# A context attention that takes its value products on four column tiles and its row sums on GpSimd

## The chip, the cores and the metric

The kernel runs on one core of one Trainium2 chip. The metric is the device time of one execution in microseconds, the median of several runs; lower is better. Each kernel is also executed once under the hardware profiler.

## What is computed

A decoder of four layers on x (4 x 256 x 128) with a context of 4 x 1601 x 96. Each layer has a self attention, a context attention and a feed-forward part, all in float32. The change touches only layer 0's context attention. Its eight heads of width 128 attend over all 4 x 1601 = 6404 context places for all 1024 queries, since the split into heads joins the batches:

```python
def _split_heads(t):
    b, n, _ = t.shape
    t = t.reshape(b, n, HEADS, DIM_HEAD)
    return t.transpose(2, 0, 1, 3).reshape(HEADS, b * n, DIM_HEAD)
...
sim = jnp.einsum('hid,hjd->hij', qh, kh) * SCALE
mean = jnp.mean(sim, axis=-1, keepdims=True)
sim = (sim - mean) * ATTN_MATRIX_SCALE + mean
attn = jax.nn.softmax(sim, axis=-1)
out = jnp.einsum('hij,hjd->hid', attn, vh)
...
return jnp.einsum('bni,iq->bnq', out, Wout) + bout
```

The mean shift drops out of the softmax; what is left is a softmax of 1.5 times the scaled scores, times the values, times Wout, added to x.

## The kernel before

The program is one list of stages. A stage (`Core.stage`) is a block in which every engine has its own hand-written instruction list; stages are separated by a barrier of all engines. Inside a stage the engines are held together by semaphores alone, and each engine takes its list in order.

`fold_weights` (L1112) multiplies, for each head, Wq with Wk and Wv with Wout, so that the big stage works on the 96 raw context features: `fold_q` turns a normalised x into a query over the context features, `fold_v` turns a mixture of context rows into the output. `ContextAhead` (L1145) holds the context in SBUF twice: as columns in thirds of 32 features, four tiles of places stacked on the 128 partitions (`c1`), and as rows, 128 places by 96 features and a 97th column of ones (`rows1`), which a memset (L1159) prepares.

`attend_all_places` (L829) is one stage. Its units of work:

- A **block** is one head and one half of the queries (512): 16 blocks. A **unit** is a block and one part of the context tiles (tiles 0 to 23 or 24 to 50): 32 units. A **group** or **slot** is four tiles of 128 places of one unit: 6 slots in the first unit of a block, 7 in the second, 208 in all. The last slot of a block has only two full tiles and one of 4 places.
- In slot s TensorE makes the **scores** of group s (L871): 12 products, four row tiles of the array side by side (32 features each) times three thirds, into banks 0 to 3. Every float32 product is two passes. ACT copies them to the **ring** of 11 slots in SBUF (L977). DVE keeps a running **maximum** over the tiles of the unit (L1039) and at its end folds it (L1045, L1047).
- The maxima are turned by TensorE (L882), reduced by DVE (L1051), spread again over all partitions by TensorE (L888) and placed by ACT (L946). Nine slots behind the scores (LAG) DVE adds them to the ring, the **shift** (L1020, L1024); ACT takes the **exponential** in place (L963).
- One slot later TensorE makes the **values** (L901): for each tile four products with 128 exponentials-by-queries as weights (loaded into the array) and the 97 columns of the rows streaming, summed over the unit in bank 4 or 5. The 97th column gives the row sums. A product of zeros (L898) opens each bank.
- At the end of a block DVE brings the two units to a common maximum, adds them and divides by the sums (L1069 to L1081), TensorE turns the result (L909), ACT copies it (L987), TensorE multiplies it by `fold_v` (L915, **mix**), DVE adds it to x (L1088).
- The three thirds of the next block's query are made (L854, L859) and copied (L953, L957) in slots 5 and 6 of a block, in banks 6 and 7.

GpSimd has no work in this stage. The order on TensorE within a slot is: scores, spread, queries, mix, values, turn of the maxima, turn of the result:

```python
for s in range(len(GROUP) + LAG + 3):
    if s < len(GROUP):
        score(s)
    ...
    if 0 <= s - LAG - 1 < len(GROUP):
        values(s - LAG - 1)
```

Two other places of the kernel matter for the prediction. In layer 0's self attention, `rotate` (from L602) multiplies query and key pieces of 128x256 by tables, eight on GpSimd (L612) and eight on DVE (L618) in the same stage, both from SBUF and with no wait between the two streams; then DVE adds them (L622). The value products of the self attention (L394) have 32 output rows each, at partitions 0, 32, 64 and 96 of one bank, and the exponentials of four heads streaming; ACT writes those exponentials at L419. In layer 2's context attention GpSimd adds 128x1601 tiles (L2780, L2785) and copies them (L2787) while DVE takes the eight largest of a row (L2810).

Of the kernel before, what the change touches and what calls it, by code (L numbers as in the profile page):

```python
# [806 lines left out]
CW = CD + 1  # L807
QUERY_AFTER = [sum(LAST[u] + 3 < FIRST[2 * n - 2] + 5 for u in range(UNITS)) for n in range(BLOCKS)]
TURN_AFTER = [1 + sum(FIRST[2 * n] + 5 <= LAST[u] + 1 for n in range(BLOCKS - 1)) for u in range(UNITS)]
# [19 lines left out]
def attend_all_places(k, c1, rows1, fold_q, fold_v, bufs):  # L829
# [4 lines left out]
    ring, top, folded_top, neg, low, spread_top, q1, first_sums, part, y, yT, gap, recip, zeros = bufs  # L834
    with k.stage() as (block, signal):
# [3 lines left out]
        evacuated, own, combined, y_turned, y_placed, mixed, added = (signal() for _ in range(7))  # L839

        @block.tensor
        def _(pe):
            def thrice(n, part):
                return fold_q[:, n // 2, part, :]

            def query(n):
                if n >= 3:
                    pe.wait_ge(added, n - 2)
                if n:
                    pe.wait_ge(query_placed, 3 * n)  # L850
                if n > 1:
                    pe.wait_ge(placed, QUERY_AFTER[n])
                for part, bank in enumerate((7, 6)):
                    pe.matmul(k.ps[:, bank, :], thrice(n, part), k.zT[:, (n % 2) * 512:(n % 2 + 1) * 512],  # L854
                              start=True, stop=True).then_inc(queried, 1)

            def query_rest(n):
                pe.wait_ge(query_placed, 3 * n + 1)
                pe.matmul(k.ps[:, 7, :], thrice(n, 2), k.zT[:, (n % 2) * 512:(n % 2 + 1) * 512],  # L859
                          start=True, stop=True).then_inc(queried, 1)  # L860
# [15 lines left out]
            def turn(u):  # L876
                pe.wait_ge(folded, u + 1)
                if u:
                    pe.wait_ge(placed, u)
                pe.wait_ge(query_placed, 3 * TURN_AFTER[u])  # L880
                for a in range(4):
                    mm = pe.transpose(k.ps[:, 6, a * P:(a + 1) * P], folded_top[:, a * P:(a + 1) * P], k.ident[:])  # L882
                mm.then_inc(turned, 1)

            def spread_out(u):
                pe.wait_ge(negated, u + 1)
                for a in range(4):
                    mm = pe.transpose(k.ps[:, 6, a * P:(a + 1) * P], neg[:, u % 4, a:a + 1].broadcast_to([P, P]), k.ident[:])  # L888
# [16 lines left out]
            def turn_rows(n):  # L905
                pe.wait_ge(combined, n + 1)
                pe.wait_ge(query_placed, 3 * min(n + 3, BLOCKS))
# [12 lines left out]
            for s in range(len(GROUP) + LAG + 3):  # L920
# [13 lines left out]
                for u in range(UNITS):  # L934
                    if s == LAST[u] + 1:
                        turn(u)
# [2594 lines left out]
```

## Time and profile before

| | |
|---|---|
| median of 3 runs | 6041.28 us (6040.34 to 6050.42) |
| the profiled execution | 6040.86 us, span 6039.1 us |
| TensorE, matmul / weight loads | 4169.8 us (69%) / 2653.2 us (44%) |
| DVE, ACT, GpSimd | 3423.9 (57%), 1894.8 (31%), 255.7 (4%) us |
| mean granted clock of TensorE | 0.82 |

The span is the time between the first and the last record of the profiled execution. Busy time counts an engine's instructions, overlapping ones once; the mean of an instruction is its own length, so that products that run side by side have means that add up to more than the busy time. "Idle before, releaser" is the time in which the engine stood still just before instructions of this group, and what ended it. PE is TensorE's matmul row, PEld its weight loads, DVE VectorE, ACT ScalarE, POOL GpSimd. PEclk is the granted clock as a share of 2.4 GHz.

### The profile page before, as it was taken

What the parts mean: (1) busy time and instruction counts of PE and PEld (TensorE: products, weight loads), DVE (VectorE), ACT (ScalarE), POOL (GpSimd) and SP (SyncE); (2) the same over time, 40 slices, a digit from 0 to 9 for tenths busy, and PEclk for the clock granted to TensorE, in tenths of its full rate; (3) what the DMA queues carried; (4) which work ended last, traced back from release to release, by engine and by line L of the source; (5) the groups of instructions that cost most, each with busy time, mean ns of one, the idle gap of its engine ahead of it and who ended that gap; (6) DMA issues with size and microseconds to landing.
All of it is one profiled execution on the core that took longest, in us unless ns stands there. A gap on an engine that the chain in (4) does not pass through costs nothing. (4 is left out here: it accounts for less than half of the span.)

```text
span 6039.1 us, 73277 instructions
## 1 busy us (share of the span) xinstructions
PE 4169.8 (69%) x28725; PEld 2653.2 (44%) x28788; DVE 3423.9 (57%) x5603; ACT 1894.8 (31%) x2350; POOL 255.7 (4%) x128
## 2 busy tenths in 40 slices
PE   4699999999992637677676761644435784727578
PEld 2367667677772613232234541322223453514356
DVE  4466666666665547666674447677774425263432
ACT  1255555555550023332331221233330231212123
POOL 1000000000000000000000001122220000000000
PEclk8899999999995869899897895566666895958789
DMA  1000000000000020000001001000000010100001
GB/s 59 1 1 1 1 1 1 1 1 1 1 1 10 0 51 1 17 1 17 17 1 56 12 2 41 0 0 0 0 0 10 1 32 12 33 16 0 7 1 35
DMA packets 19441, 67.31 MB, mean 11 GB/s; under 512 B 4753, under 2 KB 5265, under 8 KB 18354
## 3 DMA queue, kind: packets, MB, share of 16 engines
q1 hardware_dynamic: 19138, 63.09, 3.8%
q8 instruction: 211, 3.46, 0.2%
q14 instruction: 92, 0.75, 0.0%
HBM read 51.93 MB, written 1.31 MB: 9 GB/s over the span
## 5 line engine op out<-in xcount | busy, mean ns | idle before, releaser
L901 PEld LDWEIGHTS banks<-L0x_context_rows,L0x_ring 128*128 128x128 f32 x6528 | 787.2, 200 | 118.9 <-issue 117.2
L901 PE MATMUL banks<-L0x_context_rows,L0x_ring 128*128 128x97 f32 x6528 | 811.6, 285 | 0.0
L871 PE MATMUL banks<-L0x_q_context,L0x_context 32*128 32x512 f32 x4896 | 677.8, 619 | 16.3 <-ACT L0x_ring L977 15.5
L977 ACT COPY L0x_ring<-banks 128x1024 f32<-128x1024 f32 (+1 forms) x416 | 395.5, 998 | 725.1 <-PE banks L871 725.1
L1039 DVE TENSOR_TENSOR L0x_maxima<-L0x_maxima,L0x_ring 128x1024 f32<-128x1024 f32 (+1 forms) x288 | 333.8, 1192 | 296.2 <-ACT L0x_ring L977 294.6
L1020 DVE TENSOR_TENSOR L0x_ring<-L0x_ring,L0x_spread 128x2048 f32<-128x2048 f32 (+1 forms) x208 | 457.7, 2203 | 15.0 <-ACT L0x_spread L946 15.0
L1352 PE MATMUL banks<-L1x_probs,L1x_v 128*9 128x256 f32 (+1 forms) x1664 | 409.2, 385 | 4.5 <-DVE L1x_probs L1442 4.5
L1416 DVE TENSOR_REDUCE L1x_maxima<-banks 128x1 f32<-128x512 f32 (+1 forms) x512 | 265.1, 567 | 243.3 <-remote 193.7
L963 ACT ACTIVATE L0x_ring<-L0x_ring 128x2048 f32<-128x2048 f32 (+1 forms) x208 | 385.8, 1855 | 20.5 <-DVE L0x_ring L1020 20.5
L871 PEld LDWEIGHTS banks<-L0x_q_context,L0x_context 32*128 32x128 f32 x4896 | 248.7, 185 | 287.8 <-issue 242.6
L1403 ACT ACTIVATE L1x_probs<-banks 128x1024 f32<-128x1024 f32 (+1 forms) x256 | 220.9, 863 | 476.0 <-PE banks L1352 474.5
L1442 DVE SCALAR_TENSOR_TENSOR L1x_probs<-L1x_probs,L1x_floor 128x1024 f32<-128x1024 f32 (+1 forms) x256 | 260.5, 1017 | 22.5 <-ACT L1x_probs L1403 20.5
L1321 PE MATMUL banks<-L1x_keys,L1x_queries 128*128 128x512 bf16 (+1 forms) x452 | 138.0, 351 | 141.1 <-DVE L1x_maxima L1416 112.5
L199 PE MATMUL banks<-identity,z_rows 128*128 128x128 f32 x104 | 25.2, 424 | 292.8 <-PEq L75 292.8
L1352 PEld LDWEIGHTS banks<-L1x_probs,L1x_v 128*9 128x9 f32 (+1 forms) x1664 | 132.1, 91 | 214.2 <-issue 65.8
L2725 PE MATMUL banks<-L2x_k,L2x_q_batch 128*128 128x512 f32 (+1 forms) x256 | 178.7, 792 | 0.0
L2810 DVE MAX8 L2x_top<-L2x_rest 128x8 f32<-128x1601 f32 x96 | 175.6, 1829 | 3.3
L2815 DVE MATCH_REPLACE8 L2x_rest<-L2x_top,L2x_rest 128x1601 f32<-128x1601 f32 x96 | 173.9, 1811 | 0.0
L2724 PE MATMUL banks<-L2x_mask_row,ones_bf 1*128 x128 | 56.5, 441 | 151.0 <-ACT L2x_scores L2738 147.8
L199 PEld LDWEIGHTS banks<-identity,z_rows 128*128 128x128 f32 x104 | 20.4, 223 | 295.6 <-issue 295.6
L1321 PEld LDWEIGHTS banks<-L1x_keys,L1x_queries 128*128 x512 | 51.6, 102 | 204.4 <-DVE L1x_maxima L1416 170.2
L1051 DVE TENSOR_REDUCE L0x_minus_max<-banks 128x4 f32<-128x512 f32 x32 | 22.1, 692 | 208.7 <-PE banks L882 208.7
(951 smaller groups left out, 6603.3 us busy)
## 6 DMA issues: line engine op xcount, KB each, us to landing
L1x_keys<-L1x_k_parts SPq DMA_DIRECT2D x192, 50.0 KB, 2.2
L1f_expert_weights<-in_L1f_experts SPq DMA_DIRECT2D x16, 512.0 KB, 9.5
L2f_expert_weights<-in_L2f_experts SPq DMA_DIRECT2D x9, 512.0 KB, 3.5
L3a_expert_weights<-in_L3a_experts SPq DMA_DIRECT2D x9, 512.0 KB, 3.5
L3f_expert_weights<-in_L3f_experts SPq DMA_DIRECT2D x9, 512.0 KB, 3.5
L0x_context<-in_context_thirds SPq DMA_DIRECT2D x1, 2496.0 KB, 13.3
L0x_context_rows<-in_context_rows SPq DMA_DIRECT2D x1, 2448.0 KB, 22.6
L1x_contexts<-in_context SPq DMA_DIRECT2D x1, 2401.5 KB, 13.3
```

Source lines behind the costliest of these rows:

```text
L871: mm = pe.matmul(k.ps[0:height(j), i, :], c1[r, j // 4, part, 0:height(j)], q1[r, u // 2 % 2, part, :], start=part == 0, stop=part == 2)
L901: mm = pe.matmul(k.ps[:, bank, a * CW:(a + 1) * CW], ring[0:height(j), s % RING, i, a * P:(a + 1) * P], rows1[0:height(j), j, :], start=Fa ...
L963: ins = act.activation(ring[:, s % RING, 0:len(full), :], ring[:, s % RING, 0:len(full), :], ACT.Exp)
L977: act.copy(ring[0:r, s % RING, 2 * p:2 * p + len(pair), :], k.ps[0:r, 2 * p:2 * p + len(pair), :]).then_inc(copied, 1)
L1020: ins = dve.tensor_tensor(o, o, spread_top[:, u % 2, None, :].broadcast_to([P, len(full), 512]), ALU.add)
L1039: dve.tensor_tensor(o, before, ring[0:r, s % RING, 2 * p:2 * p + m, :], ALU.max).then_inc(maxed, 1)
L1321: pe.matmul(k.ps[:, 4 + i % 2, 0:m], queries[:, h, bass.ds(b * S + it * P, P)], keys[:, h // 2, c:c + m], start=True, stop=True).then_inc( ...
L1352: mm = pe.matmul(k.ps[at:at + d + 1, 6 + h % 2, 0:S], v[0:rows, j, h, :], probs[0:rows, n % 2, i, :], start=j == 0, stop=j == JT - 1)
L1403: act.activation(probs[0:rows, n % 2].rearrange("p a n -> p (a n)")[:, 0:m], k.ps[0:rows, 2 * (n % 2):2 * (n % 2) + 2, :].rearrange("p a n ...
L1416: dve.tensor_reduce(mx[:, i:i + 1], k.ps[:, 4 + i % 2, 0:CHUNKS[i % 4][1]], X, ALU.max).then_inc(reduced, 1)
L1442: dve.scalar_tensor_tensor(out=o, in0=o, scalar=1.0, in1=floor[0:rows, h % 2, None, :].broadcast_to([rows, len(js), S]), op0=ALU.min, op1= ...
L2725: mm = pe.matmul(k.ps[:, i, 0:n], qb[:, 0, h, it * P:(it + 1) * P], kT[:, c:c + n], start=False, stop=True)
```

## The change

The values swap their operands. For each of the three thirds of the 96 features, four tiles of the slot multiply side by side on four column tiles of the array: 32 columns of the context rows are the weights, the 512 exponentials of the tile stream. The results of four tiles stay on separate partitions (four partial sums of 32 features) in banks 4, 5 and 6. At a unit's end ACT copies the three banks at once (`move`), and TensorE mixes them with a `fold_v` that holds each third four times, so that the product over 128 partitions also adds the four partial sums. This is done for each unit, and DVE combines the two products of a block afterwards. The ones column is gone; GpSimd adds the exponentials of a unit over its tiles in a `tally` of 128x2048, folds it twice, and TensorE sums it over the partitions with a column of ones (`total`). ACT may not reuse a ring slot before GpSimd has added it. Queries, turns, spreads, totals and mixes share bank 7, in one order written by `last_bank_by_slot`, each waiting for the reader of the one before.

```diff
+def last_bank_by_slot(s):
+
+    middle = [("spread", u) for u in range(UNITS) if s == LAST[u] + 2]
+    behind = [("top", u) for u in range(UNITS) if s == LAST[u] + 1]
+    behind += [("sums", u) for u in range(UNITS) if s == LAST[u] + LAG + 2]
+    behind += [("mix", u) for u in range(UNITS) if s == LAST[u] + LAG + 3]
+    for part, at in enumerate((5, 8, 9)):
+        behind += [("query", 3 * (u // 2 + 1) + part) for u in range(0, UNITS - 2, 2) if s == FIRST[u] + at]
+    return middle, behind
...
+            def when_free(use):
+                if use in USE_BEFORE:
+                    kind, n = USE_BEFORE[use]
+                    released = {"spread": placed, "top": negated, "sums": noted, "mix": kept, "query": query_placed}[kind]
+                    pe.wait_ge(released, n + 1)
...
             def values(s):
                 u, js = GROUP[s]
-                bank = 4 + u % 2
                 pe.wait_ge(exped, s + 1)
-                if s == FIRST[u]:
-                    if u >= 2:
-                        pe.wait_ge(combined if u % 2 else evacuated, u // 2)
-                    pe.matmul(k.ps[:, bank, 0:4 * CW], zeros[0:1, 0:P], zeros[0:1, 0:4 * CW], start=True, stop=False)
-                for i, j in enumerate(js):
-                    for a in range(4):
-                        mm = pe.matmul(k.ps[:, bank, a * CW:(a + 1) * CW], ring[0:height(j), s % RING, i, a * P:(a + 1) * P],
-                                       rows1[0:height(j), j, :], start=False, stop=s == LAST[u] and i == len(js) - 1 and a == 3)
+                if s == FIRST[u] and u:
+                    pe.wait_ge(moved, u)
+                for c in range(3):
+                    for i, j in enumerate(js):
+                        mm = pe.matmul(k.ps[32 * i:32 * i + 32, 4 + c, :], rows[0:height(j), j, 32 * c:32 * c + 32],
+                                       ring[0:height(j), s % RING, i, :], start=s == FIRST[u], stop=s == OVER[4 * u + i])
                 mm.then_inc(summed, 1)
...
+            def total(u):
+                when_free(("sums", u))
+                pe.wait_ge(gathered, u + 1)
                 for a in range(4):
+                    mm = pe.matmul(k.ps[:, 7, a:a + 1], folded_tally[:, a * P:(a + 1) * P], k.ones[:, 0:1], start=True, stop=True)
+                mm.then_inc(totalled, 1)
+
+            def mix(u):
+                when_free(("mix", u))
+                pe.wait_ge(moved, u + 1)
                 for a in range(4):
+                    for c in range(3):
+                        mm = pe.matmul(k.ps[:, 7, a * P:(a + 1) * P], moved_out[:, c, a * P:(a + 1) * P], fold_v[:, u // 4, c, :],
+                                       start=c == 0, stop=c == 2)
                 mm.then_inc(mixed, 1)
...
             def take(s):
...
                     if s >= RING:
                         act.wait_ge(summed, s - RING + 1)
+                        act.wait_ge(tallied, tally_by(s - RING))
...
+            def move(u):
+                act.wait_ge(summed, LAST[u] + 1)
+                if u:
+                    act.wait_ge(mixed, u)
+                act.copy(moved_out[:], k.ps[:, 4:7, :]).then_inc(moved, 1)
...
+        @block.gpsimd
+        def _(pool):
+            for s in range(len(GROUP)):
+                u, js = GROUP[s]
+                before = tally_by(s - 1)
+                full = [j for j in js if height(j) == P]
+                now = ring[:, s % RING, 0:len(full), :]
+                pool.wait_ge(exped, s + 1)
+                if s == FIRST[u]:
+                    if u:
+                        pool.wait_ge(gathered, u)
+                    pool.tensor_copy(tally[:], now).then_inc(tallied, 1)
+                else:
+                    pool.wait_ge(tallied, before)
+                    pool.tensor_tensor(tally[:, 0:len(full), :], tally[:, 0:len(full), :], now, ALU.add).then_inc(tallied, 1)
...
+                if s == LAST[u]:
+                    pool.wait_ge(tallied, tally_by(s))
+                    pool.tensor_tensor(tally[:, 0:2, :], tally[:, 0:2, :], tally[:, 2:4, :], ALU.add).then_inc(half_tally, 1)
+                    pool.wait_ge(half_tally, u + 1)
+                    if u:
+                        pool.wait_ge(totalled, u)
+                    pool.tensor_tensor(folded_tally[:], tally[:, 0, :], tally[:, 1, :], ALU.add).then_inc(gathered, 1)
...
+            def note(u):
+                dve.wait_ge(totalled, u + 1)
+                dve.tensor_copy(sums[:, u % 2, :], k.ps[:, 7, 0:4]).then_inc(noted, 1)
+
+            def keep(n):
+                dve.wait_ge(mixed, 2 * n + 1)
+                dve.wait_ge(weighed, n + 1)
+                dve.tensor_tensor(part[:], product(), weight(n, 0), ALU.mult).then_inc(kept, 1)
...
             def combine(n):
...
+                dve.tensor_tensor(y[:], product(), weight(n, 1), ALU.mult).then_inc(kept, 1)
+                dve.wait_ge(kept, 2 * n + 2)
                 step(dve.tensor_tensor(y[:], y[:], part[:], ALU.add))
-                step(dve.reciprocal(recip[:], y[:, :, CD]))
...
+                step(dve.tensor_tensor(y[:], y[:], recip[:, :, None].broadcast_to([P, 4, P]), ALU.mult))
+                step(dve.tensor_tensor(xs, xs, y[:], ALU.add))
...
-                pe.matmul(k.ps[0:CD, 4 + h % 4, 0:P], heads[:, h, 2, 0:CD], heads[:, h, 3, :], start=True, stop=True).then_inc(product, 1)
+                for c in range(3):
+                    for i in range(4):
+                        mm = pe.matmul(k.ps[32 * i:32 * i + 32, 4 + h % 4, c * P:(c + 1) * P], heads[:, h, 2, 32 * c:32 * c + 32],
+                                       heads[:, h, 3, :], start=True, stop=True)
+                mm.then_inc(product, 1)
```

The queries of the next block keep their number (three products, three copies), in slots 5, 8 and 9 of a block instead of 5 and 6; DVE's add to x moves into `combine`. `layer0_context` loads the bias row and normalises before it allocates the buffers of the stage, and two of these (`part`, `y`) lie in `z`.

## Rows read from the trace of the kernel before

**Rows 1.** The page: busy time by engine, and TensorE's busy tenths in 40 slices.

```profile
PE 4169.8 (69%) x28725; PEld 2653.2 (44%) x28788; DVE 3423.9 (57%) x5603; ACT 1894.8 (31%) x2350; POOL 255.7 (4%) x128
...
PE   4699999999992637677676761644435784727578
```

**Rows 2.** Source view of L854 and L1088: count, ns min/median/max, first and last start.

```profile
L854 PE MATMUL banks<-z_columns,L0x_folded_q x64: 592/592/1192, 241.8 to 1629.6; 128*128 128x512 f32 x64
...
L1088 DVE TENSOR_TENSOR x_residual<-x_residual,banks x16: 678/681/689, 413.9 to 1828.3; 128x512 f32<-128x512 f32 x16
```

**Rows 3.** Windows: stretch, length, busy us (count) of PE, PEld, DVE, ACT, POOL; then PEclk.

```profile
242.00:305.00 63.00, 45.18 (x268) 17.40 (x272) 23.32 (x20) 24.07 (x28) 0.00 (x0) 0.85 0.00 1
250.00:256.00 6.00, 3.99 (x24) 1.65 (x24) 0.00 (x0) 1.93 (x2) 0.00 (x0) 0.76 0.00 0
400.00:800.00 400.00, 400.00 (x3117) 282.90 (x3116) 261.81 (x217) 212.89 (x196) 0.00 (x0) 0.96 0.00 1
```

**Rows 4.** Groups of the stage: busy us, mean ns, idle before and releaser.

```profile
L901 PE MATMUL banks<-L0x_context_rows,L0x_ring 128*128 128x97 f32 x6528 | 811.6, 285 | 0.0
...
L871 PE MATMUL banks<-L0x_q_context,L0x_context 32*128 32x512 f32 x4896 | 677.8, 619 | 16.3 <-ACT L0x_ring L977 15.5 <-ACT L0x_q_context L957 0.7
L1020 DVE TENSOR_TENSOR L0x_ring<-L0x_ring,L0x_spread 128x2048 f32<-128x2048 f32 (+1 forms) x208 | 457.7, 2203 | 15.0 <-ACT L0x_spread L946 15.0
L977 ACT COPY L0x_ring<-banks 128x1024 f32<-128x1024 f32 (+1 forms) x416 | 395.5, 998 | 725.1 <-PE banks L871 725.1
...
L915 PE MATMUL banks<-L0x_folded_v,L0x_y_columns 96*128 96x128 f32 x128 | 19.5, 297 | 0.7 <-ACT L0x_y_columns L987 0.7
...
L909 PE MATMUL banks<-identity,L0x_y 128*96 128x128 f32 x64 | 10.1, 282 | 2.5 <-DVE L0x_y L1081 2.5
```

**Rows 5.** Windows over the stage, of the instructions on L0x_maxima, then on L0x_spread.

```profile
242.00:1829.00 1587.00, 470.73 (x416) 0.95 0.00 1
...
242.00:1829.00 1587.00, 467.17 (x224) 18.78 (x32) 0.95 0.00 1
```

**Rows 6.** Timeline of one slot: start, length in us, engine, what.

```profile
1009.13 2.86 PE L871 MATMUL banks<-L0x_q_context,L0x_context 32*128 32x512 f32 x24
...
1011.92 3.81 PE L901 MATMUL banks<-L0x_context_rows,L0x_ring 128*128 128x97 f32 x32
...
1013.84 1.92 ACT L963 ACTIVATE L0x_ring<-L0x_ring 128x2048 f32<-128x2048 f32 x1
```

**Rows 7.** Timeline in the self attention: L419's exponentials, L394's column tiles.

```profile
110.49 1.45 ACT L419 ACTIVATE L0a_probs<-banks 128x1536 f32<-128x1536 f32 x1 [8.11 <-PE banks L374]
...
112.00 0.86 PE L394 MATMUL banks<-L0a_probs,L_v 128*32 128x128 f32 x24 [1.21 <-ACT L0a_probs L419]
```

**Rows 8.** Groups of GpSimd over the whole span.

```profile
L2780 POOL TENSOR_TENSOR L2x_exp_all<-L2x_exp_all,L2x_exp_rest 128x1601 f32<-128x1601 f32 x28 | 100.1, 3575 | 560.5 <-ACT L2x_exp_top L2768 560.5
...
L612 POOL TENSOR_TENSOR L_raw<-L_raw,L_attn_weights 128x256 f32<-128x256 f32 x16 | 12.3, 805 | 45.1 <-PEq L75 45.1
L2787 POOL COPY L2x_heads_mean<-L2x_exp_scaled 128x1601 f32<-128x1601 f32 x8 | 12.2, 1520 | 13.8 <-ACT L2x_exp_scaled L2755 13.8
```

**Rows 9.** Source view of L2810.

```profile
L2810 DVE MAX8 L2x_top<-L2x_rest x96: 1828/1829/1830, 3846.9 to 4474.0; 128x8 f32<-128x1601 f32 x96
```

**Rows 10.** Timeline of `rotate`, narrow windows: DVE alone first, then both.

```profile
61.40 0.42 DVE L618 TENSOR_TENSOR L_raw<-L_raw,L_attn_weights 128x256 f32<-128x256 f32 x1 [1.07 <-PEq L75]
...
61.40 0.76 DVE L618 TENSOR_TENSOR L_raw<-L_raw,L_attn_weights 128x256 f32<-128x256 f32 x2 [1.07 <-PEq L75]
...
61.94 0.72 POOL L612 TENSOR_TENSOR L_raw<-L_raw,L_attn_weights 128x256 f32<-128x256 f32 x1 [42.28 <-PEq L75]
...
71.59 0.82 POOL L612 TENSOR_TENSOR L_raw<-L_raw,L_attn_weights 128x256 f32<-128x256 f32 x1
...
71.83 0.85 DVE L618 TENSOR_TENSOR L_raw<-L_raw,L_attn_weights 128x256 f32<-128x256 f32 x1
...
72.37 0.82 POOL L612 TENSOR_TENSOR L_raw<-L_raw,L_attn_weights 128x256 f32<-128x256 f32 x1
```

More of the change, by code:

```diff
@@ L826, in height, with attend_all_places @@
     return min(P, ALL - j * P)
-def attend_all_places(k, c1, rows1, fold_q, fold_v, bufs):
-    ring, top, folded_top, neg, low, spread_top, q1, first_sums, part, y, yT, gap, recip, zeros = bufs
+def attend_all_places(k, c1, rows, fold_q, fold_v, bufs):
+    (ring, top, folded_top, neg, low, spread_top, q1, part, y, gap, recip, tally, folded_tally, moved_out, sums,
+     scaled_sums) = bufs
     with k.stage() as (block, signal):
@@ L838, in attend_all_places, with tally_by @@
         queried, query_placed, lowest, differed, weighed = (signal() for _ in range(5))
-        evacuated, own, combined, y_turned, y_placed, mixed, added = (signal() for _ in range(7))
+        tallied, half_tally, gathered, totalled, noted, moved, mixed, kept, own = (signal() for _ in range(9))
+        def tally_by(s):
+            return sum(TALLIES[0:s + 1])
         @block.tensor
         def _(pe):
-            def thrice(n, part):
-                return fold_q[:, n // 2, part, :]
-            def query(n):
[L847 to L859, printed above, removed]
+            def when_free(use):
[3 more added lines that the diff above has]
+                    pe.wait_ge(released, n + 1)
+            def query(n):
+                when_free(("query", n))
+                b = n // 3
+                pe.matmul(k.ps[:, 7, :], fold_q[:, b // 2, n % 3, :], k.zT[:, (b % 2) * 512:(b % 2 + 1) * 512],
                           start=True, stop=True).then_inc(queried, 1)
@@ L920, in _ @@
-            for s in range(len(GROUP) + LAG + 3):
+            use = {"spread": spread_out, "top": turn, "sums": total, "mix": mix, "query": query}
+            for part in range(3):
+                query(part)
+            for s in range(SLOTS):
+                middle, behind = last_bank_by_slot(s)
                 if s < len(GROUP):
                     score(s)
-                for u in range(UNITS):
-                    if s == LAST[u] + 2:
-                        spread_out(u)
-                    if s == FIRST[u] + 5 and u % 2 == 0 and u + 2 < UNITS:
-                        query(u // 2 + 1)
-                    if s == FIRST[u] + 6 and u % 2 == 0 and u + 2 < UNITS:
-                        query_rest(u // 2 + 1)
-                    if s == LAST[u] + LAG + 3 and u % 2:
-                        mix(u // 2)
+                for kind, n in middle:
+                    use[kind](n)
@@ L932, in _ @@
                 if 0 <= s - LAG - 1 < len(GROUP):
                     values(s - LAG - 1)
-                for u in range(UNITS):
-                    if s == LAST[u] + 1:
-                        turn(u)
-                    if s == LAST[u] + LAG + 2 and u % 2:
-                        turn_rows(u // 2)
+                for kind, n in behind:
+                    use[kind](n)
         @block.scalar
@@ L1083, in add, with product @@
-            def add(n):
-                dve.wait_ge(mixed, n + 1)
-                xs = k.x[:, 4 * (n % 2):4 * (n % 2) + 4, :].rearrange("p a c -> p (a c)")
-                if n >= 2:
-                    dve.wait_ge(added, n - 1)
-                dve.tensor_tensor(xs, xs, k.ps[:, 7, :], ALU.add).then_inc(added, 1)
-            for s in range(len(GROUP) + LAG + 3):
+                return gap[:, n % 2, part, :, None].broadcast_to([P, 4, P])
+            def product():
+                return k.ps[:, 7, :].rearrange("p (a e) -> p a e", a=4)
@@ L1091, in _ @@
+            for s in range(SLOTS):
                 for u in range(UNITS):
@@ L1168, in _ @@
                 sp.dma_start(self.c1[:].rearrange("p g t j -> p (g t j)"), k.dram["context_thirds"]).then_inc(self.here, 16)
-                sp.dma_start(self.rows1[:, :, 0:CD], k.dram["context_rows"]).then_inc(self.here, 16)
+                sp.dma_start(self.rows[:], k.dram["context_rows"]).then_inc(self.here, 16)
 def layer0_context(k):
```

141 lines of the change are left out of this document (58 added, 83 removed).

## The prediction, made before the change was run

> **What bounds the kernel now.** The page comes first: TensorE is the busiest engine (4169.8 us, 69%), and in slices 3 to 12 its digits are 9 [rows 1]. That stretch is the stage the diff rewrites. It runs from its first query product at 242 us to its last residual add, which starts at 1828.3 and takes 0.69 [rows 2]: 1587 us. The windows tell what TensorE does in it: 400.00 of 400 us busy at a granted clock of 0.96, with DVE at 262, ACT at 213 and GpSimd at 0 [rows 3]. The groups of the same stretch name the two parts: the value products (L901) hold 811.6 us, the scores (L871) 677.8, over 208 slots 3.90 and 3.26 us each, while ACT sits idle for 725 us until scores come [rows 4]. In one slot at full clock the scores take 2.86 us and the values 3.81 [rows 6]. So a slot costs about 7.5 us because TensorE needs that. DVE's work beside it is about 4.7 us a slot, ACT's 3.9 [rows 3].
>
> **The values on four column tiles.** 16 full-width products (32 passes) a slot become 12 products (24 passes) of 512 columns, each on 32 columns of the array. They help only if four run side by side. The kernel already has such a product, L394 in the self attention: 24 passes of 128 columns in 0.86 us, 0.036 us each [rows 7]; 128 full-width passes of 128 columns (L915) take 19.5 us, 0.152 each [rows 4]. So they do run side by side. The nearest row for 512 columns is the score product, four row tiles in 24 passes, 2.86 us. I take that: 3.81 becomes 2.86 at full clock, 208 x 0.95 = 198 us of TensorE work saved; by the busy means (3.90 against 3.26) it is 134.
>
> **The outputs mixed per key part.** Twelve products (24 passes) for each of 32 units replace four for each of 16 blocks: 768 passes of 0.152 us are 117 us. Gone are L915 (19.5) and the transposes L909 (10.1) [rows 4]; the 32 zero products have no row here and I put them at L909's 10. The four one-column sums of a unit are 256 passes bound by their weight loads: L915's 0.152 is an upper price, nothing (all loads hidden) a lower one, so 0 to 39 us; I take 33, near the upper, since the loads have nothing to hide under. TensorE nets out at -198+117-40+33 = -88 us, or -24 by the means. That is all this change can give while TensorE sets the slot.
>
> **ACT and the one bank.** ACT gains 32 copies of 128x1536 out of PSUM; L419 writes 128x1536 in 1.45 us [rows 7], so 46 us. With 725 us of idle [rows 4] it stays covered; without that cover the price would be 46. All other products now share bank 7, each waiting for the previous reader, and TensorE's queue holds the next scores behind those waits. A reader of 128x512 takes 0.68 us (L1088) [rows 2], and the order leaves each most of a slot, so I cost the waits at nothing while the readers run on time; what a late reader costs is a rival below.
>
> **The small moves.** The memset of the rows and its stage go, the fold of weights issues 24 passes in place of 2 for each of eight heads, at most 0.86 us more each: between a few us less and 7 more. I take +2. Loading rows and the bias is the same work in another order. The three queries of a block stay.
>
> **The sums on GpSimd, and this decides.** Before, the row sums came free as the 97th column of the values. Now GpSimd adds up the exponentials. Its prices, alone: an addition of 128x1601 takes 3575 ns, of 128x256 805, a copy of 128x1601 1520 [rows 8]. The slope is (3575-805)/1345 = 2.06 ns, so 2048 elements cost 4.49 us, 1024 2.39, 512 1.34, and a copy of 2048 1.94. A block of 13 slots has two copies, ten full additions, the last slot's 1024 and 512, and two folds of 1024+512: 3.9+44.9+3.7+7.5 = 60.0 us, 960 in all over 16 blocks, 4.6 a slot. Beside a slot of 7 us that would be hidden.
>
> But it does not run beside DVE. At 61 to 77 us both engines work through independent streams of two-input instructions on SBUF, with no wait between them (L612 and L618). DVE alone does one in 0.42 us and two in 0.76, so it starts one every 0.34. Once GpSimd runs, its starts are at 71.59 and 72.37, and DVE's instruction lasts 0.85 instead of 0.42 [rows 10]. They alternate, one pair in 0.78 us, where 0.34 for DVE and 0.72 for a lone GpSimd would be 1.06 in a row: they exclude each other but for 0.28 us of start and end. DVE's instructions with one SBUF input are not touched: MAX8 in layer 2 kept within 1828 to 1830 ns in all 96 cases [rows 9], beside the 48 long additions of the same stretch [rows 8]. In our stage nearly all of DVE's time is in two-input instructions: those on the maxima 470.7 us, the shifts 467.2 [rows 5], together 938; the new combine adds three of 0.68 a block, 33. So 971.
>
> The shared resource then needs 971+960 = 1931 us, less 0.28 for each of GpSimd's 18 x 16 = 288 instructions, 81: 1850 us, 8.9 a slot, more than TensorE's 7. Can it stay filled? After a shift ends, its exponential (1.92 [rows 6]) runs while DVE does two maxima (2.3); then GpSimd's addition is ready and takes about 4.2; then comes the next shift, 2.2. That closes at 8.7 us with no hole. While the first nine slots fill the ring GpSimd has nothing: of the 63 us from 242 to 305 DVE uses 23.3 [rows 3], so 40 stay empty. The last sums and mix add some 5. The stage takes 1850+40+5 = 1895 instead of 1587: +308, with the 2 above **+310**.
>
> The Trainium skill (SBUF — State Buffer, Who interferes with whom) says that a DVE instruction with two SBUF inputs and a GpSimd one that reads SBUF hold a port pair exclusively, for the whole instruction. The alternation agrees, but the measured overlap of 0.28 us does not fit "whole"; by the rule alone the time would be 81 us higher, 6432.
>
> **Bounds of that price.** Below: if only what a pair's 0.78 leaves after DVE's 0.34 is GpSimd's, it holds 0.44 for 256 elements, 1.72 ns each; 25088 added elements a block give 43.1 us, with the copies 47, so 752+971+45 = 1768, +183: 6224. Above: no overlap (+81) and additions scaled by 2048/1601 to 4.57 us (+13): 6445. I stay between, since the overlap is measured and the slope rests on the long rows, which are nearest in size.
>
> **The sum.** The profiled execution took 6040.86 us, 0.4 below the median of 6041.28. 6041+310 = **6351 us**.
>
> **The rivals.**
> *No contention that counts, TensorE still sets the slot: faster.* For it: the alternation was seen on 256-element instructions alone, and DVE idles some 2.8 us a slot, into which GpSimd's additions could fall. Against it: the two need 8.9 us a slot together, and 2.8 of idle does not hold 4.2. It decides where the two need less than about 7 us a slot together. It gives -88 or -24 us: 5953 to 6017, say 5980. 0.07.
> *GpSimd's tail at each unit.* TensorE waits for the folded sums, two slots after a unit's last exponential, before it may take the next scores. The fold is 3.7 us for each of 32 units and alternates with DVE; if TensorE, and behind it ACT and DVE, stand still for it and nobody fills the port, 119 us come on top: 6470. For it: one queue for all. Against it: I count 12 us from that exponential to the fold's end, and two slots are 17.8. 0.10, half of it below my upper end.
> *The clock.* TensorE will be busy some 6.2 of 8.9 us. In the fill of the ring, 3.99 of 6 us busy, the granted clock had a mean of 0.76 [rows 3], a mixture of the levels 1.2 and 2.4 GHz. If it stayed there, a slot's 6.7 us at 0.96 would take 8.5, still under 8.9; only near 0.6 would it pass, at 10.7: 208 x 1.8 = 374 on top, 6725. But then TensorE would be full, and a full TensorE holds 0.96 now. 0.06.
> *The change does not do what it says*: column tiles of 512 columns one after another, each pass at a row-tile group's 2.86/6 = 0.48 us: 11.4 us of values, a slot over 14, above 7300. L394 speaks against it. 0.01.
> *Half a contention*, by which the stage ends where it began: 0.03.
>
> **How the numbers follow.** My forecast has 0.73. The range reaches from its lower bound to the tail rival: 6220 to 6470. A measurement of this kernel can tell about 0.2% from no change. Faster 0.07, same 0.02, slower 0.91.
>
> **What the profile after would show.** GpSimd some 950 us or more busy in the stage. The mean of the shifts or of the maxima 1 us or more above today's (2203 ns for L1020 [rows 4]), because they wait inside the instruction, or GpSimd's additions above 4.5 us. The values below 700 us at the same clock. TensorE below 80% busy, waiting for ACT's copies, and those for GpSimd's or DVE's part. Wrong would be: DVE's means unchanged beside a busy GpSimd, or a slot below 7.5 us.

## The result, and the profile after

The changed kernel takes 6419.07 us (median of four, 6411.73 to 6422.23) beside 6040.81 for the one before: a ratio of 1.0621, interval 1.0603 to 1.0639, 378 us more. The forecast was +310, 6351; its range, 6220 to 6470, holds the result. The page after, to be laid beside [rows 1]:

```profile
PE 4283.2 (67%) x28132; PEld 2144.0 (33%) x28132; DVE 4148.8 (65%) x5650; ACT 1937.6 (30%) x2366; POOL 1488.7 (23%) x415
...
PE   4688888888888535667667676254443675717678
...
DVE  4499899899899664667667544677776334263432
...
POOL 1065666666666500000000000122220000000000
```

TensorE's nines have become eights and DVE's digits have risen to eights and nines, over 11 slices instead of 10. The windows of the same stretch as in [rows 3], and three narrow ones that are used further down:

```profile
400.00:800.00 400.00, 346.34 (x2349) 120.48 (x2342) 356.19 (x178) 183.05 (x165) 267.24 (x62) 0.89 0.00 1
1012.00:1014.00 2.00, 1.97 (x6) 0.28 (x6) 2.00 (x2) 2.00 (x3) 1.95 (x1) 0.97 0.01 4
1014.00:1021.00 7.00, 7.00 (x13) 0.73 (x12) 5.31 (x4) 2.16 (x2) 7.00 (x1) 0.50 0.00 0
1023.00:1028.00 5.00, 5.00 (x25) 1.93 (x24) 0.00 (x0) 0.59 (x1) 4.79 (x3) 0.55 0.00 0
```

TensorE was busy for 400 of 400 us and is now at 346; DVE went from 262 to 356. The groups of the stage that answer to [rows 4], with GpSimd's full additions:

```profile
L1025 POOL TENSOR_TENSOR L0x_tally<-L0x_tally,L0x_ring 128x2048 f32<-128x2048 f32 x160 | 838.4, 5240 | 560.3 <-ACT L0x_ring L962 552.3 <-POOL L0x_tally L1022 0.4
...
L910 PE MATMUL banks<-L0x_ring,L0x_context_rows 128*32 128x512 f32 x4896 | 727.6, 665 | 182.9 <-ACT L0x_moved_values L990 131.7 <-ACT L0x_ring L965 31.2 <-ACT L0x_ring L962 19.1
L885 PE MATMUL banks<-L0x_q_context,L0x_context 32*128 32x512 f32 x4896 | 726.6, 665 | 15.6 <-ACT L0x_ring L978 14.9 <-ACT L0x_q_context L956 0.7
L1049 DVE TENSOR_TENSOR L0x_ring<-L0x_ring,L0x_spread 128x2048 f32<-128x2048 f32 (+1 forms) x208 | 647.5, 3114 | 3.0 <-ACT L0x_spread L950 2.5
L1068 DVE TENSOR_TENSOR L0x_maxima<-L0x_maxima,L0x_ring 128x1024 f32<-128x1024 f32 (+1 forms) x288 | 453.5, 1609 | 158.2 <-ACT L0x_ring L978 158.2
L1068 DVE TENSOR_TENSOR L0x_maxima<-L0x_ring 128x1024 f32<-128x1024 f32 x64 | 309.5, 4875 | 44.4 <-ACT L0x_ring L978 43.2
L926 PE MATMUL banks<-L0x_folded_v,L0x_moved_values 128*128 128x128 f32 x768 | 95.9, 282 | 0.3 <-DVE L0x_sums L1098 0.3
L1086 DVE TENSOR_TENSOR L0x_lowest<-L0x_minus_max 128x4 f32<-128x4 f32 x16 | 32.1, 2008 | 0.0
```

No DVE instruction got more work, yet the shift's mean went from 2203 ns to 3114 (+190 us over 208) and the first maxima of a unit hold 4875 each. Read such a mean as a wait inside the instruction: DVE has started and stands. GpSimd's full additions, priced at 4.49 us alone, stand too: 5.24 on the mean, where the shortest of the 160 lasts 4.53. In the timeline of DVE and GpSimd one sees both kinds:

```profile
996.83 10.72 POOL L1025 TENSOR_TENSOR L0x_tally<-L0x_tally,L0x_ring 128x2048 f32<-128x2048 f32 x2 [6.04 <-ACT L0x_ring L962]
998.94 9.69 DVE L1068 TENSOR_TENSOR L0x_maxima<-L0x_ring 128x1024 f32<-128x1024 f32 x2 [1.33 <-ACT L0x_ring L978]
...
1012.05 9.46 POOL L1025 TENSOR_TENSOR L0x_tally<-L0x_tally,L0x_ring 128x1024 f32<-128x1024 f32 x1 [4.50 <-ACT L0x_ring L965]
1012.57 2.27 DVE L1049 TENSOR_TENSOR L0x_ring<-L0x_ring,L0x_spread 128x2048 f32<-128x2048 f32 x1
1014.77 2.34 DVE L1068 TENSOR_TENSOR L0x_maxima<-L0x_maxima,L0x_ring 128x1024 f32<-128x1024 f32 x2
1017.04 2.27 DVE L1049 TENSOR_TENSOR L0x_ring<-L0x_ring,L0x_spread 128x2048 f32<-128x2048 f32 x1
```

At 999 two maxima that need 2.3 us together take 9.7 beside two additions. At 1012 it is GpSimd that stands: its addition of 1024 elements (2.39 us by the forecast's slope) lasts 9.46. It stands as long as DVE has one two-input instruction directly behind the other, until 1019.31, and ends 2.20 us after the last of them.

The last lines also point at something that the forecast had not seen. TensorE's timeline around them:

```profile
415.83 5.93 PE L910 MATMUL banks<-L0x_ring,L0x_context_rows 128*32 128x512 f32 x18
...
1003.87 2.78 PE L910 MATMUL banks<-L0x_ring,L0x_context_rows 128*32 128x512 f32 x24
...
1012.03 9.46 PE L910 MATMUL banks<-L0x_ring,L0x_context_rows 128*32 128x512 f32 x18 [1.53 <-ACT L0x_ring L965]
...
1023.43 4.87 PE L885 MATMUL banks<-L0x_q_context,L0x_context 32*128 32x512 f32 x24
1028.22 2.78 PE L910 MATMUL banks<-L0x_ring,L0x_context_rows 128*32 128x512 f32 x24
```

The last tile of the context is 4 places high. The slot that ends in it has 18 passes instead of 24, yet takes 9.46 us instead of 2.78, and the granted clock, 0.97 in its first 2 us, is 0.50 in the next 7 (1.2 GHz in place of 2.4) and still 0.55 in the scores behind it, which need 4.87 us instead of 2.86. From 1019.31 on DVE gets nothing new and is idle for 10.07 us. In every other block the same slot takes 5.93 us (415.83, at a granted clock of 1.00), still twice a full one. What that is worth had to be measured.

### The profile page after: what moved, and what is told of

It reads as the page before. It is cut to its first block and busy times, and to the rows that moved or that the text cites. A ratio compares the mean times of both kernels' runs of the same rounds, so it can differ in the third digit from the quotient of the medians.

```text
span 6420.5 us, 72658 instructions
## 1 busy us (share of the span) xinstructions
PE 4283.2 (67%) x28132; PEld 2144.0 (33%) x28132; DVE 4148.8 (65%) x5650; ACT 1937.6 (30%) x2366; POOL 1488.7 (23%) x415
## 5 line engine op out<-in xcount | busy, mean ns | idle before, releaser
L1025 POOL TENSOR_TENSOR L0x_tally<-L0x_tally,L0x_ring 128x2048 f32<-128x2048 f32 (+1 forms) x176 | 982.8, 5584 | 628.9 <-ACT L0x_ring L962 552.3
L910 PE MATMUL banks<-L0x_ring,L0x_context_rows 128*32 128x512 f32 x4896 | 727.6, 665 | 182.9 <-ACT L0x_moved_values L990 131.7
L885 PE MATMUL banks<-L0x_q_context,L0x_context 32*128 32x512 f32 x4896 | 726.6, 665 | 15.6 <-ACT L0x_ring L978 14.9
L1049 DVE TENSOR_TENSOR L0x_ring<-L0x_ring,L0x_spread 128x2048 f32<-128x2048 f32 (+1 forms) x208 | 647.5, 3114 | 3.0 <-ACT L0x_spread L950 2.5
L962 ACT ACTIVATE L0x_ring<-L0x_ring 128x2048 f32<-128x2048 f32 (+1 forms) x208 | 384.8, 1850 | 575.9 <-DVE L0x_ring L1049 499.9
L1068 DVE TENSOR_TENSOR L0x_maxima<-L0x_maxima,L0x_ring 128x1024 f32<-128x1024 f32 (+1 forms) x288 | 453.5, 1609 | 158.2 <-ACT L0x_ring L978 158.2
L978 ACT COPY L0x_ring<-banks 128x1024 f32<-128x1024 f32 x400 | 385.9, 1015 | 440.6 <-PE banks L885 420.1
L910 PEld LDWEIGHTS banks<-L0x_ring,L0x_context_rows 128*32 128x32 f32 x4896 | 157.0, 119 | 714.0 <-issue 629.3
L1068 DVE TENSOR_TENSOR L0x_maxima<-L0x_ring 128x1024 f32<-128x1024 f32 x64 | 309.5, 4875 | 44.4 <-ACT L0x_ring L978 43.2
L1349 PE MATMUL banks<-L1x_keys,L1x_queries 128*128 128x512 bf16 (+1 forms) x512 | 151.7, 356 | 136.4 <-DVE L1x_maxima L1444 112.5
L2808 POOL TENSOR_TENSOR L2x_exp_all<-L2x_exp_all,L2x_exp_rest 128x1601 f32<-128x1601 f32 x28 | 100.1, 3574 | 558.6 <-ACT L2x_exp_top L2796 558.6
```

Of the source, the lines that this page charges most:

```text
L885: mm = pe.matmul(k.ps[0:height(j), i, :], c1[r, j // 4, part, 0:height(j)], q1[r, u // 2 % 2, part, :], start=part == 0, stop=part == 2)
L910: mm = pe.matmul(k.ps[32 * i:32 * i + 32, 4 + c, :], rows[0:height(j), j, 32 * c:32 * c + 32], ring[0:height(j), s % RING, i, :], start=s ...
L962: ins = act.activation(ring[:, s % RING, 0:len(full), :], ring[:, s % RING, 0:len(full), :], ACT.Exp)
L978: act.copy(ring[:, s % RING, 2 * p:2 * p + len(pair), :], k.ps[:, 2 * p:2 * p + len(pair), :]).then_inc(copied, 1)
L1025: pool.tensor_tensor(tally[:, 0:len(full), :], tally[:, 0:len(full), :], now, ALU.add).then_inc(tallied, 1)
L1049: ins = dve.tensor_tensor(o, o, spread_top[:, u % 2, None, :].broadcast_to([P, len(full), 512]), ALU.add)
```

## The experiments

**Without the adding up.** Theory: a port that DVE and GpSimd share sets the slot. Rivals: TensorE's new order, or the waits on bank 7. GpSimd's tally is left out; a constant stands in for the row sums, so the result itself is of no use.

```diff
-                        act.wait_ge(tallied, tally_by(s - RING))
...
-                    pool.tensor_tensor(tally[:, 0:len(full), :], tally[:, 0:len(full), :], now, ALU.add).then_inc(tallied, 1)
...
+            for u in range(UNITS):
+                pool.wait_ge(exped, LAST[u] + 1)
...
+                pool.memset(folded_tally[:], 1.0).then_inc(gathered, 1)
```

> The kernel after with all of GpSimd's tally left out: no copy, no addition, no fold; the row sums are replaced by a memset of 128x512 per unit, and ACT no longer waits for GpSimd. Everything else (column tiles, mix per unit, one bank) stays. Theory A, DVE and GpSimd exclude each other: with nothing on GpSimd that reads, L1049 and L1068 go back to 2.20 and 1.19 us and TensorE sets the slot; 5990 to 6060 us. Rival B, the order on bank 7 and the waits of TensorE's queue are what costs: above 6300 us.

Measured: 5997.9 us (5995.66 to 5998.73), ratio 0.993 (0.9914 to 0.9947). The shift, now at line 1029, is back where it was, and TensorE has no gap between 400 and 1600 us:

```profile
L1029 DVE TENSOR_TENSOR L0x_ring<-L0x_ring,L0x_spread 128x2048 f32<-128x2048 f32 (+1 forms) x208 | 457.9, 2203 | 15.6 <-ACT L0x_spread L950 15.0
```

```profile
400.00:1600.00 1200.00, 1200.00 (x9008) 438.90 (x9006) 815.44 (x697) 685.85 (x616) 13.13 (x25) 0.98 0.00 1
```

That is in the range of the theory and far from the rival's 6300. Everything else in the change gains 42 us, and the adding up costs 421.

**As long, but only writing.** Is it GpSimd's length (ACT and TensorE wait for its semaphores) or its reading? The additions become memsets of about the same length in all, with every wait kept; the sums are not computed.

```diff
-                    pool.tensor_tensor(tally[:, 0:len(full), :], tally[:, 0:len(full), :], now, ALU.add).then_inc(tallied, 1)
...
+                if s != FIRST[u]:
+                    write(tally[:])
+                    write(tally[:, 0:2, :])
+                write(tally[:])
```

> The kernel after with GpSimd as long busy as by its additions, at the same places and with the same waits and signals, but with memsets, which read nothing: 2048+1024+2048 elements in place of an addition of 2048, about 4.5 us. The sums are not computed. Theory A (what costs is the reading of two engines side by side): within 20 us of the run without additions. Rival C (GpSimd's length itself costs, since ACT waits for it to free a ring slot and TensorE for its folds): within 50 us of the 6419 us of the kernel after.

Measured: 6009.7 us, ratio 0.9954 (0.9937 to 0.997), 12 us above the run without additions, as the theory had it. Group and windows:

```profile
L1019 POOL MEMSET L0x_tally<- 128x2048 f32 (+2 forms) x640 | 950.6, 1485 | 708.5 <-ACT L0x_ring L962 657.3 <-ACT L0x_ring L965 15.7 <-POOL L0x_folded_tally L1019 6.8
...
L1053 DVE TENSOR_TENSOR L0x_ring<-L0x_ring,L0x_spread 128x2048 f32<-128x2048 f32 (+1 forms) x208 | 457.9, 2203 | 15.5 <-ACT L0x_spread L950 15.0
```

```profile
400.00:1600.00 1200.00, 1200.00 (x8974) 438.40 (x8976) 812.78 (x694) 682.93 (x614) 786.95 (x564) 0.97 0.00 1
```

GpSimd is busy for 787 of 1200 us (782 in the changed kernel), with the same semaphores before ACT and TensorE, and DVE's shift keeps its 2203 ns to the nanosecond. It is the reading. The Trainium skill (SBUF — State Buffer, Who interferes with whom) says the same: a DVE instruction with two SBUF inputs contends with a GpSimd one that reads SBUF, not with one that only writes.

**The kernel before with one addition a slot.** If reading alone does it, an addition that nobody waits for must slow the old kernel.

```diff
+            for s in range(len(GROUP)):
+                pool.wait_ge(exped, s + 1)
+                pool.wait_ge(beside_done, s + 1)
+                pool.tensor_tensor(beside[:], beside[:], beside[:], ALU.add).then_inc(beside_done, 1)
```

> The kernel before with one addition of 128x2048 on GpSimd per slot, on a buffer of its own; it waits for the slot's exponential, and nobody waits for it. Theory A: the port is asked for 938 us by DVE and 208 x 4.49 by GpSimd, less 0.28 a pair, plus 40 of start: 1854 in place of 1587, so about 6310 us (6220 to 6420). Rivals B and C, by which order and waits cost: 6041 us, unchanged.

Measured: 6242.39 us, ratio 1.0337 (1.032 to 1.0354): +202, in the range but below the forecast. The groups show that the shifts now stand:

```profile
L1015 POOL TENSOR_TENSOR L0x_beside<-L0x_beside 128x2048 f32<-128x2048 f32 x208 | 843.7, 4056 | 935.0 <-ACT L0x_ring L963 893.9 <-ACT L0x_ring L966 39.9
...
L1028 DVE TENSOR_TENSOR L0x_ring<-L0x_ring,L0x_spread 128x2048 f32<-128x2048 f32 (+1 forms) x208 | 810.2, 3897 | 4.8 <-ACT L0x_spread L946 4.8
```

An addition whose inputs are the same tile is cheaper than the 4.49 that I had put in: the shortest lasts 3.60 us, the median 3.71; the mean of 4.06 has waits in it. With 3.71 the sum is 938 (DVE) + 772 - 58 + 40 = 1692 us of stage. It took 1790 (244.0 to 2033.8), because for 106 us, beside the 40 in which the ring fills, neither engine was in an instruction that reads through the port (DVE's with two SBUF inputs, GpSimd's that read). Two errors of opposite sign put the time into my range. What the run shows is that reading alone is enough: nobody waits for these additions, and the shifts rise from 2203 to 3897 ns.

**A whole last tile in the changed kernel.** The 4-place tile is filled to 128 places with copies of context columns; their rows are zero and they stay out of the sums.

```diff
-    return min(P, ALL - j * P)
+    return P
...
-                full = [j for j in js if height(j) == P]
+                full = [j for j in js if j < AT - 1]
```

> The kernel after with the last context tile, 4 places high, made 128 high: 124 places come a second time in the columns of the scores, with zero rows for the values, and GpSimd adds only the 4 real ones, so that the result is unchanged. Theory D: products of 4 rows or 4 columns between those of 128 do not run side by side with them, which costs some 10 us of TensorE per block while the port stays empty: 6270 to 6350 us. Rival (the port is always asked for, TensorE's time is hidden): within 20 us of 6419.

Measured: 6389.44 us (6383.37 to 6396.13), only 30 below the changed kernel. That is a miss: above the theory's 6350 and a little outside the rival's 20. Windows, and a place where both engines queue for the port:

```profile
400.00:1600.00 1200.00, 952.95 (x7122) 378.98 (x7114) 1173.22 (x537) 544.10 (x481) 752.94 (x185) 0.90 0.00 1
```

```profile
1025.62 2.27 DVE L1049 TENSOR_TENSOR L0x_ring<-L0x_ring,L0x_spread 128x2048 f32<-128x2048 f32 x1
1027.82 2.35 DVE L1068 TENSOR_TENSOR L0x_maxima<-L0x_maxima,L0x_ring 128x1024 f32<-128x1024 f32 x2
...
1029.92 4.64 POOL L1025 TENSOR_TENSOR L0x_tally<-L0x_tally,L0x_ring 128x2048 f32<-128x2048 f32 x1 [5.38 <-ACT L0x_ring L962]
...
1030.09 4.50 DVE L1108 TENSOR_TENSOR L0x_scaled_sums<-L0x_sums,L0x_gap 128x8 f32<-128x8 f32 x1
```

DVE is now busy or standing for 1173 of 1200 us (98%) and TensorE for 953. TensorE's holes at the narrow tile were mostly spare time; I had counted DVE's idle time there as if the port could be filled with other work. The 1895 us of stage that the prediction had summed up meet 1940 here (243.3 to 2183.7).

The last two lines show both ends of a stand. The addition starts 0.25 us before the maxima end (1027.82 + 2.35) and lasts 4.64, where the forecast's price is 4.49 and the shortest addition of this run takes 4.54; DVE's 128x8 instruction, 0.16 us long when nothing holds it, is done 0.03 after the addition. The overlap at both ends together is then 0.23 us by the one length and 0.28 by the other, which leaves the prediction's 0.28 standing.

**A whole last tile in the kernel before.**

```diff
-    return min(P, ALL - j * P)
+    return P
...
-                pool.memset(self.rows1[:], 1.0)
...
-                sp.dma_start(self.rows1[:, :, 0:CD], k.dram["context_rows"]).then_inc(self.here, 16)
+                sp.dma_start(self.rows1[:], k.dram["context_rows"]).then_inc(self.here, 16)
```

> The kernel before, with the last context tile made 128 places high as in the run on the kernel after (124 places a second time in the columns, zero rows and a zero in the column of ones for them; the result is unchanged, and the memset of the ones is gone). Theory D: the slot with the tile of 4 places takes 6.85 us of scores and 5.6 to 6.3 of values, with whole tiles at most 2.9 and 3.8; about 6 us for each of 16 blocks, TensorE being the bound: 5945 us (5925 to 5980). Rival: a tile of 4 costs what a tile costs, 6041.

Measured: 5921.63 us beside 6036.65 in the same series, ratio 0.9819 (0.9806 to 0.9833): 115 us saved, a little more than the range allowed, and faster than both kernels of this case. Here TensorE sets the slot, so all of the tile's price comes back. The kernel before shows it in the timeline and the windows of TensorE:

```profile
899.84 6.85 PE L871 MATMUL banks<-L0x_q_context,L0x_context 32*128 32x512 f32 x18
906.62 6.29 PE L901 MATMUL banks<-L0x_context_rows,L0x_ring 128*128 128x97 f32 x32
```

```profile
899.90:903.90 4.00, 4.00 (x15) 0.76 (x14) 1.61 (x1) 0.00 (x0) 0.00 (x0) 1.00 0.00 0
903.90:906.70 2.80, 2.80 (x8) 0.41 (x7) 0.64 (x1) 1.01 (x1) 0.00 (x0) 0.70 0.00 0
906.70:912.00 5.30, 5.30 (x26) 5.30 (x27) 5.19 (x5) 2.39 (x2) 0.00 (x0) 0.51 0.00 0
```

and with whole tiles:

```profile
400.00:1600.00 1200.00, 1200.00 (x10027) 872.78 (x10020) 832.46 (x669) 679.39 (x614) 0.00 (x0) 1.00 0.00 1
```

The scores of the narrow slot take 6.85 us where a full slot's take 2.86, the granted clock falls from 1.00 to 0.70 within them and to 0.51 behind them, and the full slot of values that follows needs 6.29 instead of 3.81: (6.85 - 2.86) + (6.29 - 3.81) = 6.5 us in this block. In ten of the 16 blocks this excess is 6.4 to 6.5 us, in the others 7.8 to 8.1: 113 together, of the 115. My expectation had about 6 in each. With whole tiles the clock is 1.00 throughout. The 0.96 of [rows 3], which I read as TensorE's state when full, was the mean of 1.00 and of these dips.

**Maxima out of the banks.** If two SBUF inputs are what DVE is held for, maxima with one input in PSUM must be free of GpSimd. The changed kernel with whole tiles (6389.44 us) gets this edit on top:

```diff
+                    pe.wait_ge(maxed, 2 * sum(t != FIRST[GROUP[t][0]] for t in range(s)))
...
+                now = k.ps[0:r, 2 * p:2 * p + m, :]
...
-                dve.tensor_tensor(o, before, ring[0:r, s % RING, 2 * p:2 * p + m, :], ALU.max).then_inc(maxed, 1)
+                dve.tensor_tensor(o, before, now, ALU.max).then_inc(maxed, 1)
```

> The kernel after with whole tiles, and DVE's running maximum taken from the scores in PSUM in place of the ring, so that it has one SBUF input; TensorE waits for it before the next scores. Theory A: 409 us of DVE's maxima stop excluding GpSimd; the port is asked for 562+960-81 us and DVE's one-input work, some 1540 with the start, about what TensorE needs: 5960 to 6060 us, 5990 likeliest, with the maxima back at 1.2 us each. Rival C (GpSimd's length and waits cost): above 6250 us. Rival B (TensorE stands behind DVE's maximum): 6100 to 6200.

Measured: 6147.5 us (6143.47 to 6153.69), 242 below its base. Groups and timeline:

```profile
L886 PE MATMUL banks<-L0x_q_context,L0x_context 32*128 32x512 f32 x4896 | 663.4, 665 | 196.2 <-DVE L0x_maxima L1070 192.1 <-ACT L0x_ring L979 3.4 <-ACT L0x_q_context L957 0.7
L1050 DVE TENSOR_TENSOR L0x_ring<-L0x_ring,L0x_spread 128x2048 f32<-128x2048 f32 (+1 forms) x208 | 653.5, 3143 | 15.7 <-ACT L0x_spread L951 15.2
...
L1070 DVE TENSOR_TENSOR L0x_maxima<-L0x_maxima,banks 128x1024 f32<-128x1024 f32 (+1 forms) x288 | 331.0, 1186 | 140.2 <-ACT L0x_ring L979 139.9
```

```profile
998.61 5.94 DVE L1050 TENSOR_TENSOR L0x_ring<-L0x_ring,L0x_spread 128x2048 f32<-128x2048 f32 x1
...
1006.96 2.86 PE L886 MATMUL banks<-L0x_q_context,L0x_context 32*128 32x512 f32 x24 [2.10 <-DVE L0x_maxima L1070]
```

The maxima, 1726 ns on the mean in the run that this edit starts from, are at 1186 (1192 in the kernel before), while the shifts, still with two SBUF inputs, stay long, at 3143. So it is the number of SBUF inputs that decides, instruction by instruction. The time missed the theory's 5960 to 6060 and lies in the range of rival B, for the wait that the edit brings: the banks are free only after the maxima, these stand behind a shift that stands for GpSimd, and TensorE is idle for 192 us.

**Both removed: no adding up, whole tiles.** The first and the fourth edit together; again the row sums are not computed.

```diff
-    return min(P, ALL - j * P)
+    return P
...
+                pool.memset(folded_tally[:], 1.0).then_inc(gathered, 1)
```

> The run without additions, with whole tiles; the row sums are not computed. It tells what TensorE alone would take in this change. Theory D: per block the slot with the tile of 4 falls by about 4 us of scores and 6.6 of values: 100 to 170 us below the 5998 of the run without additions, 5830 to 5900. Rival: unchanged within 15 us.

Measured: 5853.28 us, ratio 0.9697 (0.9682 to 0.9712), 145 below the run without additions, in the expected range. That is the floor of the change, 68 us below the kernel before with the same tiles (5921.63); any place for the sums must cost less than that. TensorE is full again (1198 of 1200 us, clock 1.00).

**The adding up on DVE.** The same additions, with whole tiles, moved from GpSimd to DVE's queue, behind the shift of each slot and before its maxima; each adds the slot before:

```diff
-        def _(pool):
-            for s in range(len(GROUP)):
...
+            def count(s):
...
+                    dve.tensor_tensor(tally[:, 0:len(full), :], tally[:, 0:len(full), :], now, ALU.add).then_inc(tallied, 1)
...
+                    count(s - LAG - 1)
```

> The kernel after with whole tiles and the whole tally moved from GpSimd to DVE, same instructions, each one slot after its exponential. Theory A: DVE needs 971+55 us as before and some 510 for 160 additions at 2.2 us, the copies and folds; with the fill of the ring about 1600 us, DVE being the bound: 6050 us (6010 to 6120), well under the 6389 with GpSimd. Rival: any tally beside the rest costs what GpSimd's did, 6300 or more.

Measured: 5976.75 us, ratio 0.99 (0.9885 to 0.9915), below the expected 6010 to 6120.

```profile
L1102 DVE TENSOR_TENSOR L0x_tally<-L0x_tally,L0x_ring 128x2048 f32<-128x2048 f32 (+1 forms) x176 | 384.7, 2186 | 0.1
...
L1099 DVE COPY L0x_tally<-L0x_ring 128x2048 f32<-128x2048 f32 x32 | 39.0, 1220 | 0.0
```

```profile
400.00:1600.00 1200.00, 1107.39 (x9086) 437.81 (x9090) 1192.86 (x925) 702.99 (x612) 0.00 (x0) 1.00 0.00 1
```

The engine that already has the most two-input work does GpSimd's as well, and the kernel is 413 us faster than with the helper: a full addition takes 2.28 us on DVE (the row's 2186 ns mixes in 16 of half the size) and 4.5 on GpSimd. DVE is full (1193 of 1200), so this costs 123 above the floor and stays 55 behind the kernel before with whole tiles. The forecast was too high: 1600 us of stage, 1536 of them DVE's work, where it took 1527 with DVE busy for 1468. The copies are 31 of these 68, since I had priced a copy as an addition (2.2 us) and it takes 1.22; the rest isn't taken apart.

## Why the prediction was right, and where its sizes were off

*TensorE sets the slot before*: right, and the 115 us of the whole tile show it again.

*Values on four column tiles*: right, a full slot takes 2.78 us where 2.86 was assumed. Without the adding up the values are 662.2 us instead of 811.6, -149, between my -134 and -198, but the narrow tile is in both figures. With whole tiles on both sides they are 581.1 instead of 769.3, -188, close to the -198 of full slots.

*Mix, sums, moves*: the mix takes 95.9 us (forecast 117: 0.125 a pass, L915 was too dear a row), the one-column sums 37.0 (33), ACT's copies 45.8 (46). All of the change but the adding up gives -42 us (-68 with whole tiles on both sides), between the forecast's -24 and -88. The one bank costs nothing visible without the adding up: TensorE is busy for all of 1200 us.

*The shared port decides*: right, and shown from three sides (reading against writing, two SBUF inputs against one, an unrelated addition in the old kernel). The price, +308 for the stage, was too small by 72: the stage took 1967 us (245.3 to 2212.6) instead of 1895. Outside it the program grew by 1 us where I had 2.

Of the 72, 27 are the narrow tile, measured by taking it away (1967 against 1940; 30 of the kernel's time); it was there to be read in the timeline of before. The other 45 can be found in the trace of the run with whole tiles, if one adds up the time in which at least one of the two engines is in an instruction that reads through the port:

| us of stage | forecast | whole tiles | changed kernel |
|---|---|---|---|
| port in use, or waited for | 1850 | 1854 | 1863 |
| unused while the ring fills | 40 | 44 | 44 |
| unused later | 5 | 42 | 60 |

So the port time was right within 1%; DVE's part of it, 971 us in the forecast, is 969 in the run without additions. That the result, 6419, lies nearer to the 6432 of full exclusion is chance: without any overlap the port would have been needed for 1931 us, not 1863. "That closes at 8.7 us with no hole" is the step that failed: the forecast allowed 5 us of unused port behind the fill, and there are 42. In 30 of these DVE is in an instruction without two SBUF inputs: the reduction of the turned maxima out of PSUM (L1080, 16 us), the product that is weighted out of PSUM (L1112, 11) and the reciprocals (L1110, 3); 7 are the end of the stage. GpSimd can only add behind an exponential, which is behind a shift of DVE, so a step of DVE that needs no port can leave both waiting; that this order is the reason is argued from the coincidence in time, and no run took these steps away. DVE's queue isn't one shift and two maxima per slot without exception.

*The rivals*: no contention is out. GpSimd's tail is small, TensorE waits 22.9 us for the folded sums before L918, not 119. The clock is at 0.89 from 400 to 800 us but doesn't decide, since TensorE had room. It costs where TensorE is full, in the kernel before.

*The signs named in advance*: the means of DVE and GpSimd rose as foretold, and a slot takes 9.5 us. The values stayed above the 700 us that I had set (727.6, though not at the same clock), and TensorE is busy 87% of the time and not below 80. Both go back to the narrow slot, in which it counts as busy at half the clock: with whole tiles the values are 640 us and TensorE is busy for 953 of 1200 (79%).

## What to carry to other kernels

Before you give elementwise work to an idle GpSimd, add up DVE's instructions with two SBUF inputs and GpSimd's reading ones as if they were on one engine, and compare the sum with the slot: here 971 + 960 us against 1587, while the same additions on DVE cost 413 us less than on its helper. Then look for the steps of either engine that leave that shared time unused: here it was 42 to 60 us where the sum had 5. Where DVE has PSUM to read from, one input there takes the instruction out of that sum, at the price of a bank held longer. And look at the slot with the odd tile on its own: a mean over 208 slots hid that one tile of 4 places in 51 cost 1.9% of the kernel.

## What the runs showed that I had not expected

Among products that run side by side, a tile of 4 rows or columns does not run beside its two full neighbours. In TensorE's weight loads the narrow ones come alone, 0.84 us and, at the low clock, 1.66 us after the full ones:

```profile
1012.03 0.14 PEld L910 LDWEIGHTS banks<-L0x_ring,L0x_context_rows 128*32 128x32 f32 x4 [2.36 <-ACT L0x_ring L965]
...
1013.01 0.13 PEld L910 LDWEIGHTS banks<-L0x_ring,L0x_context_rows 4*32 4x32 f32 x2 [0.84 <-issue]
...
1014.03 0.19 PEld L910 LDWEIGHTS banks<-L0x_ring,L0x_context_rows 128*32 128x32 f32 x4 [0.89 <-issue]
1015.88 0.18 PEld L910 LDWEIGHTS banks<-L0x_ring,L0x_context_rows 4*32 4x32 f32 x2 [1.66 <-issue]
```

By the Trainium skill (TensorEngine Tiling (Array Packing), Key Properties) changing the tiling mode, not just the tile, drains TensorE. Loads that alternate with a gap would fit that; that the narrow tile changes the mode is my reading, and no run here tests it. What the trace adds is the price: 18 passes take 5.93 us in every other block; in the eight between them 9.3 to 10.2, with the next scores at 4.8 to 5.1 us, and in the one looked at here the granted clock falls to 0.50. In the values of the kernel before, where the four narrow products of a slot stand together at its end, they cost nothing of the kind: the 24 passes from 978.76 on take 3.08 us.

Size does not protect a DVE instruction: L1086 works on 128x4 and takes 2008 ns on the mean, 16 times over, and in the run with whole tiles the 128x8 at 1030.09 stood for 4.50 us; one that met no addition, L1108 at 1045.27 of the changed kernel, lasts 0.16. And the two engines don't always take turns at the port, as they did in `rotate`: with DVE's instructions back to back, GpSimd's stood from 1012 until they ended.
